# Moving the product with Wo and one state scan across a loop's jump, the norm ahead of the scores, and halving one accumulating DMA

## The reference, cut to what matters

```python
x = x + xattn(ctx, ctx, layernorm(x), mask)      # 64 sequences, 32 rows each, 257 keys, 16 heads of 32
x = x + mamba(layernorm(x))
x = x + ffn(layernorm(x))                        # with quantised activations and weights

# mamba: xz = x @ in_proj; causal convolution of 4 taps, silu; B, C, dt from x_proj; then for each
# of 1024 channels with 16 states, over 32 steps:
h = exp(dt * A) * h + (dt * x) * B
y = sum_n(h_n * C_n) + D * x ;   y = y * silu(z) ;   out = y @ out_proj
```

## Time and profile before

| | us |
|---|---|
| median of 3 runs | 2045.06 |
| lowest and highest run | 2039.28 and 2049.81 |
| profiled execution, its time | 2040.54 |
| profiled execution, its span | 2038.6 |
| PE busy | 1877.5 (92%) |
| DVE busy | 1788.9 (88%) |
| ACT busy | 1624.1 (80%) |
| POOL busy | 544.1 (27%) |

### The profile page before, as it was taken

How to read it: one execution, slowest core, us unless ns; L and a number is a source line. 1 busy time by engine, 2 the same in 40 slices (tenths; PEclk the granted TensorE clock), 3 DMA queues, 4 the chain that set the end, 5 groups by cost and what they waited for, 6 DMA issues and landing times. The chain is left out here.

```text
span 2038.6 us, 44073 instructions
## 1 busy us (share of the span) xinstructions
PE 1877.5 (92%) x14989; PEld 1298.0 (64%) x15004; DVE 1788.9 (88%) x2193; ACT 1624.1 (80%) x4441; POOL 544.1 (27%) x435
## 2 busy tenths in 40 slices
PE   7898999999999999999899999999898999577799
PEld 5576666767676666666676767666666657376444
DVE  1546999999989999999999999999999998989788
ACT  3358888897979888888889797888888898777483
POOL 1001324231423232242413142423324241301014
PEclk9999999999999999999999999999999999789899
DMA  8623444433443433343444435344344434420214
GB/s 288 220 81 90 92 107 90 105 85 97 90 118 74 113 82 84 105 99 102 88 106 91 97 77 129 68 102 100 80 107 90 106 84 106 97 81 11 73 41 145
DMA packets 97677, 203.85 MB, mean 100 GB/s; under 512 B 17380, under 2 KB 40308, under 8 KB 92280
## 3 DMA queue, kind: packets, MB, share of 16 engines
q1 hardware_dynamic: 76376, 133.32, 21.1%
q0 software_dynamic: 21024, 67.12, 18.1%
HBM read 116.12 MB, written 17.18 MB: 65 GB/s over the span
## 5 line engine op out<-in xcount | busy, mean ns | idle before, releaser
L1485 ACT ACTIVATE dA<-dt,A_sb 128x124 f32<-128x124 f32 x2048 | 618.3, 399 | 5.1 <-DVE dt L1816 5.0
L1867 DVE TENSOR_TENSOR_SCAN hb<-dA,hb 128x2048 f32<-128x2048 f32 x118 | 526.3, 4460 | 9.7 <-ACT dA L1485 6.4
L1008 PE MATMUL bank<-ctxT,wk_sb 128*128 128x256 f32 x2048 | 468.8, 384 | 20.2 <-ACT Q L1362 15.7
L1019 PE MATMUL bank<-wv_sb,ctxT 128*128 128x512 f32 x1024 | 469.9, 599 | 2.3 <-ACT ctxT L1295 2.3
L1008 PEld LDWEIGHTS bank<-ctxT,wk_sb 128*128 128x128 f32 x2048 | 380.7, 191 | 89.1 <-ACT Q L1362 21.3
L1594 POOL DMA_DIRECT2D hb<-hb x117 | 105.2, 899 | 822.8 <-DVE hb L1873 797.3
L1019 PEld LDWEIGHTS bank<-wv_sb,ctxT 128*128 128x128 f32 x1024 | 186.3, 191 | 190.5 <-issue 187.7
L1862 DVE TENSOR_TENSOR hb<-u,BC 128x2048 f32<-128x2048 f32 x118 | 270.0, 2288 | 6.6 <-DVE u L1829 2.6
L1873 DVE TENSOR_TENSOR hb<-hb,BC 128x2048 f32<-128x2048 f32 x117 | 268.6, 2296 | 1.5
L1117 PE MATMUL bank<-xn2T,win_sb 128*128 128x128 f32 x2048 | 242.9, 281 | 0.7 <-ACT xn2T L1391 0.7
L1117 PEld LDWEIGHTS bank<-xn2T,win_sb 128*128 128x128 f32 x2048 | 241.2, 198 | 3.4 <-issue 1.3
(11 more groups left out here) (170 smaller groups left out, 2493.3 us busy)
## 6 DMA issues: line engine op xcount, KB each, us to landing
hb<-hb POOLq DMA_DIRECT2D x117, 512.0 KB, 5.1
ctx_sb<-in_ctx_dram SPq DMA_DIRECT2D x64, 512.0 KB, 3.8
BC<-bcd_dram SPq DMA_DIRECT2D x32, 1024.0 KB, 7.4
maskb<-in_mask_Bx1x1xS_fk_dram SPq DMA_DIRECT2D x64, 128.5 KB, 3.5
wstage<-in_L_ffn_w_dram SPq DMA_DIRECT2D x4, 2048.0 KB, 11.1
x_sb<-in_x_dram SPq DMA_DIRECT2D x16, 256.0 KB, 4.0
win_sb<-in_L_attn_in_proj_w_dram SPq DMA_DIRECT2D x1, 4096.0 KB
bo_sb<-bias_dram SPq DMA_DIRECT2D x64, 64.0 KB, 2.1
```

Source lines behind the costliest of these rows:

```text
L1008: last = pe.matmul(bank[6 + j][:, (m % 2) * KF:(m % 2 + 1) * KF], wk_sb[:, c, m * P:(m + 1) * P], ctxT[:, c, :], start=(c == 0), stop=(c = ...
L1019: last = pe.matmul(bank[h][:], ctxT[:, c, h * P:(h + 1) * P], wv_sb[:, c, :], start=(c == 0), stop=(c == DC - 1))
L1485: last = act.activation(dA[:, c % 2, n * BT:(n + 1) * BT, 1:], dt[:, c, :].rearrange("p (b s) -> p b s", s=S)[:, :, 1:], ACT.Exp, scale=A_ ...
L1867: ins = dve.tensor_tensor_scan(flat, dA[:, c % 2].rearrange("p n s -> p (n s)"), flat, 0.0, ALU.mult, ALU.add)
```

## The change

Five edits. (1) `wo_product` moves from the end of b = 3 to the start of the next interval's b = 0, behind the jump, and in `tail` to the front. (2) Step 20 of `CHAIN`, the scan (5, 1), moves from the end of the interval to a new place "x" behind the jump; DVE now has x1's sum, the norm's statistics and then this scan before the score passes. (3) `mamba_rows` moves from behind the normalisation to right behind the exponentials. (4) At b = 3 Q's product and copies move ahead of the decays of place "m". (5) For the last chunk, c = 7, the DMA adds only four of the eight states, and DVE adds the other four with one more instruction, before it waits for the DMA.

```diff
-        FINISH = {(0, "a"): range(21, 22), ...
+        FINISH = {(0, "x"): range(20, 21), (0, "a"): range(21, 22), ...
-                 (3, "e"): range(19, 21)}
+                 (3, "e"): range(19, 20)}
...
         def tail(part):
+            part.wo_product(LAST, 0)
             part.weights_transpose(range(0, 8))
             part.x1_write(LAST)
             part.mamba_norm(LAST)
+            part.scans(PREV, range(20, 21))
...
                     if b == 0 and front:
+                        part.wo_product(tm, DC * (g + 1))
                         part.x1_write(tm)
+                        part.mamba_norm(tm)
+                    if b == 0:
+                        place("x")
...
                     if here:
                         part.scores(g, ta, b, to)
-                    if b == 0 and front:
-                        part.mamba_norm(tm)
...
                     if here:
                         part.softmax(g)
+                    if b == 0 and front:
+                        part.mamba_rows(tm)
                     if b == 0:
                         place("a")
+                    if b == 3 and here and more:
+                        part.q_product(ta + 1)
+                        part.q_spread(ta + 1)
                     place("m")
...
-                    if b == 3 and here and more:
-                        part.q_product(ta + 1)
-                        part.q_spread(ta + 1)
...
-                    if b == 0 and front:
-                        part.mamba_rows(tm)
...
-                    if b == 3 and here:
-                        part.wo_product(ta, keys)
...
-                            pool.dma_start(hb[:, c % 2, 0:NS // 2, :], hb[:, c % 2, NS // 2:NS, :], accum_op=ALU.add
-                                           ).then_inc(hb_added[c % 2], 16)
+                            first = NS // 4 if c == IC - 1 else 0
+                            pool.dma_start(hb[:, c % 2, first:NS // 2, :], hb[:, c % 2, NS // 2 + first:NS, :],
+                                           accum_op=ALU.add).then_inc(hb_added[c % 2], 16)
...
+                    done = (2 * IC + 1) * t + 2 * c
+                    n = NS // 4
+                    if c == IC - 1:
+                        dve.tensor_tensor(tile[:, 0:n, :], tile[:, 0:n, :], tile[:, 2 * n:3 * n, :], ALU.add
+                                          ).then_inc(sum_step, 1)
+                        done += 1
+                        dve.wait_ge(sum_step, done)
                     dve.wait_ge(hb_added[c % 2], 16 * (IC // 2 * t + c // 2 + 1))
-                    n = NS // 4
-                    done = 2 * IC * t + 2 * c
```

More of the change, by code:

```diff
@@ L334, in perceiver_kernel @@
         DONE[IC - 1, 3] += 1
-        FINISH = {(0, "a"): range(21, 22), (0, "b"): range(22, 26), (0, "c"): range(26, 28),
+        FINISH = {(0, "x"): range(20, 21), (0, "a"): range(21, 22), (0, "b"): range(22, 26), (0, "c"): range(26, 28),
                   (1, "a"): range(28, 29), (1, "t"): range(29, 31), (1, "p"): range(31, 32)}
```

## The result

The changed kernel takes 2072.10 us (median of 4 runs, 2070.45 to 2073.34), beside 2045.62 (4 runs, 2039.28 to 2049.81) for the kernel before: a ratio of 1.0132, 95% interval 1.0104 to 1.0160. It is slower, as forecast, by 26 us where the sum had 23. The profiled execution took 2073.24 us, its span 2071.3; the execution profiled before took 2040.5, so the traces compared here are 32.7 us apart.

The account below looks back on a forecast made before the run. A chain through DVE at the jump, the convolution and PE was taken to bound the kernel. 11 x (2.6 - 0.75) + 3 = 23 us on 2040.5 gave 2063.5, or 2068 from the median; predicted 2065, range 2046 to 2081.

Parts of the forecast that it names:

- The circle: Chain setting the pass: DVE from b = 2 through jump and convolution, then PE to b = 2; five segments, 110.4 us.
- Rival C: PE, not the chain through DVE, sets the pass: 33 us faster, 2012 us; chance 0.08.
- lost cover: At the jump, the scan no longer hides DVE's branch: first score pass 2.2 to 3.0 us later, taken as 2.6.
- worst case: Latest forecast start of the first score pass after the jump: R + 9.7, 3.0 us later than before.
- R: End of DVE's product (5, 0), just before the jump; 1001.89 us in the earlier trace.
- second delay: DVE's later instruction wait after a jump, forecast to end about 6.2 us after the branch, at R + 4.0.
- bare branch: PE's 3.3 us branch, partly unhidden before Wo's product: PE idles up to 1.5 us, at no cost to the pass.
- win-back: Earlier normed rows absorb PE's lateness ahead of the convolution: 0.6 to 0.8 us a pass won, 0.75 in the sum.
- P: Start of DVE's first score pass after the jump: R + 6.74 on average before, forecast R + 8.9 to R + 9.7.
- Passages without a jump: Two passages between intervals without a jump: first score pass from R + 5.3 to R + 6.6, 1.4 later, 3 us.
- Rival B: Other block borders keep the second delay from standing ahead of the scan: 2050 us, within 0.5%; chance 0.17.
- Rival D: Early rows win nothing because PE's new idle times lower its clock, with P at its worst: 2079 us; chance 0.13.

Follow-up runs that it names:

- the last kernel above: Kernel before with 16 semaphore increments ahead of DVE's loop, early Q copies, halved DMA sum, norm ahead of score passes, early normed rows: 2040.29 us, 0.9994.
- The run with the late branch: Changed kernel with DVE made to wait for the end of its own product (5, 0) before it jumps: 2083.95 us, 1.0210.
- the shifted change: Changed kernel with sixteen semaphore increments added on DVE, once, ahead of its loop: 2036.31 us, 0.9978.
- the kernel with four increments: Kernel before with four semaphore increments added on DVE ahead of its loop: 2035.46 us, 0.9975.

## Why the prediction was right

- **Bound.** The circle held: four of its five segments came out within 0.1 us, and the runs with (4) or (5) alone took away waits for nothing. Rival C, in which PE sets the pass, is excluded by these and by the last kernel above, which is slower with PE's wait gone.
- **(2), lost cover.** The mechanism was right, and its term of +2.6 us a pass was mis-sized; it is 10.38 - 6.74 = +3.64. That is also beyond the prediction's worst case, R + 9.7. I took DVE's delays as they had been, 3.5 and 6.2 us after the branch. They came at 5.0 and 7.8, so the aggregation began at R + 5.7, where the second delay had been put to end at R + 4.0. What followed took 4.6 us (forecast 4.9). DVE's idle time before x1's sum is 3.06 us, not 1.5. In the kernel before, ACT's branch came at 999.4 and its next instruction at 1002.2, so its delay was all but over when DVE's branch came at 1002.0; I didn't ask when ACT's would come in the changed order. The run with the late branch shows that the extra 1.5 us goes with the place of DVE's branch; that it is ACT's beside it is the likelier of two readings. Undoing (2) returns 2.7 of the 3.64.
- **(1).** PE stands idle for 1.71 us before Wo's product. With the product ahead of the jump it is 0.94, for ACT's copy, so the bare branch adds 0.8. It costs nothing here, as forecast; at one jump of the shifted change it does.
- **(3).** The win-back was put at 0.75 us a pass and is 0.82: the convolution ends at P + 21.84 to 21.93 in all passes, where six of eleven had 23.2 to 23.3. The prediction had these down to PE's lateness and did not ask where that came from. The kernel before, PE in the pass of the earlier trace rows:

```profile
904.00:909.00 5.00, 4.69 (x28) 4.72 (x29) 4.86 (x2) 4.65 (x14) 2.13 (x3) 0.66 0.76 146
906.36 8.24 PE L1117 MATMUL bank<-xn2T,win_sb 128*128 128x128 f32 x64
```

  In just those six passes the granted clock stands at 0.5 for 3.41 us from about P + 8 on, and the in-projection takes 7.9 to 8.6 us instead of 7.38. PE had waited some 3 us for the normed rows just before, but so it had in the passes in which the clock stayed. In the changed kernel the clock falls there in nine of eleven passes, for 3.4 to 6.8 us, and the in-projection takes 8.2 to 9.4; yet it begins at P + 6.9 instead of P + 8.8 or later, and DVE does not wait. Without edit (3), the kernel with four increments has no fall there and no late convolution. So what (3) is worth hangs on where the clock falls. PE's wait at the turn fell to 2.9 us only, not to about 1. ACT wrote the rows right behind the exponentials, at P + 2.4, as forecast; but P itself is later, and PE had run out of work by P + 0.6 (P + 3.9 before). This was off the circle.
- **(4), (5).** Zero, shown by themselves.
- **Passages without a jump.** P - R went from 5.25 to 6.66, +1.41 as forecast (1.4); there are three of them, not two.
- **Sum.** 11 x (3.64 - 0.82) = 31.0 in the loop, 2.8 in the first intervals, 1.2 at the head, -2.3 at the end: 32.7. The forecast for the loop was 20.4; the medians, 26 us apart, hide part of this miss.
- **Rival B** came close to another truth: other borders do take the second delay away, and the first too, but these edits left the second delay ahead of the scan.
- **Rival D** had its clock right and its price wrong. The mean granted clock of the run fell from 0.975 to 0.966 and the late P is beyond its worst case, but the falls lie where PE is off the circle: its segment stays at 35.42 us and the win-back of (3) came.

## What to carry to other kernels

Before you remove an engine's waits, follow the pass round to the stretch in which another engine has no gap: a wait beside that stretch is worth nothing, and an instruction put in it costs its full time. Keep long work queued ahead of a jump on the engine that sets the pass: here 4.7 us of it covered a delay of 3.1 to 4.1 us. Where a loop's instructions nearly fit the blocks held, a few cheap instructions ahead of it can make the jump free, and orders should be compared at one such alignment: here the alignment was worth 24 us on one order and some 31 on the other by the ratios, about as much as the whole change cost.

## What was not expected of the hardware

- DVE's jump costs 3.1 to 5.4 us to its first instruction and 2.4 to 3.2 more at the next border, or 0.3 us and nothing, by where its body of 292 records starts: 16 increments made it free, 4 did not. "Mostly hidden", as the same section of the Trainium skill has it for crossing into a next block, doesn't hold soon after a jump in these traces.
- A 128x1 operation on POOL took 4.20 us while DVE's scan ran, where the same operation took 0.23 us in the kernel before; the two of the same norm behind the scan took 0.57 and 0.26 us.
- One stretch of 3.41 us at a granted clock of 0.5 lengthens a pass by 1.5 us where PE sets the time, and by nothing where PE is off the circle. Over the twelve executions of one kernel the time goes with it, 2034.6 us at 0.980 and 2044.0 at 0.976.
